# Attention with turned sine weights: TensorE transposes two of a batch's four weight units into the score banks, and the scores accumulate on them

## The chip, the core and the metric

The kernel runs on one NeuronCore of a Trainium2 chip. The metric is device time in microseconds (us) of one execution. Five engines work side by side, each through its own instruction queue in order: TensorE (PE, matmuls and transposes), VectorE (DVE), ScalarE (ACT), GpSimd (POOL) and SyncE (SP, which here only issues DMAs). They meet at semaphores. PSUM, the accumulator memory, has eight banks of 128 x 512 f32.

## What is computed

The input is 16 batches of 256 tokens of width 128. The kernel is one transformer block: attention with eight heads and a second, "quantum" similarity, a small feed-forward part, and a mixture of eight experts behind it. The change touches the attention scores only:

```
qq, kq = Q @ Wc2q + bc2q, K @ Wc2q + bc2q          # 8 numbers per head and token
fid    = (qq @ kq.T) / max(|qq| * |kq|, 1e-8)      # a cosine
qw     = fid * (1 + 0.1 * sin(pi * fid))
cw     = (Q @ K.T) / sqrt(16)
probs  = softmax(0.5 * qw + 0.5 * cw)
heads  = probs @ V
```

## The kernel before

Attention runs batch by batch, 16 times (`batches`). A batch has eight heads, taken two at a time: four units n = 0 to 3, each of them two heads x 256 keys x 256 queries, which is a 128 x 1024 f32 tile. Four such tiles of a batch stand in SBUF as `W[par][:, n, :]` (the trace calls them `big`); `par` is the parity of the batch. Three kinds of unit go through PSUM:

- **max**: Q K^T with queries as rows (`max_unit`, L1210). DVE reduces it over the keys (`top`, L1686), and the row maxima travel over POOL (`split_max`), TensorE (`turn_max`, L1200), ScalarE (`take_max`, L861) and two DMAs into two extra rows of the query stack. Max units belong to the next batch, b + 1.
- **cos**: the cosine, with keys as rows (`cos_unit`, L1328). ScalarE takes the sine into W (L897), DVE forms W = (W + 10) * cos (`weight`, L1735).
- **log**: the score product, keys as rows, with the maxima taken off through the two extra rows (`logit_unit`, L1341). DVE adds W = 0.05 * W + product (`logits`, L1765), ScalarE takes the exponential in place (`exp`, L901), and TensorE multiplies by V (`pv`, L1354, two calls per batch, each on two units of the batch before).

A unit needs two PSUM banks, and there are three such pairs, used in turn: unit number k stands in `slot[k % 3]`. The list `units` fixes the order for a batch b: cos 0, cos 1, cos 2, cos 3, log 0, max 0, log 1, max 1, log 2, log 3, max 2, max 3, with the max units those of b + 1. TensorE waits in `unit` with `pe.wait_ge(unit_free, k - 2)` until DVE has read unit k - 3. Twelve units and three slots: the slot of max 1 is the one of log 0, the slot of max 3 is the one of log 2. The slots of log 0 and log 2 were used before by cos 1 and by max 0.

Each engine's order in a batch is written out by hand (`body` of each engine):

- TensorE: cos 0, 1, 2, `turn_max(b, 1)`, cos 3, `make_qk` for b + 2 (L1180), log 0, max 0, log 1, `turn_u` (L1193), pv 0 of b - 1, max 1, log 2, pv 1 of b - 1, log 3, `turn_max(b + 1, 0)`, `heads_back` (L1366, four 128 x 128 f32 transposes), max 2, max 3.
- VectorE: four weights, then logits 0, top 0, logits 1, top 1, logits 2, logits 3, heads (L1772, L1775), top 2, top 3.
- ScalarE: sin 0, sin 1, `take_max(b, 1)`, sin 2, sin 3, `take_qk` (L848, after `make_qk`), exp 3 of b - 1, exp 0, `take_u`, exp 1, `heads_out` (L906, after pv 1), `take_max(b + 1, 0)` (after log 3 and the transposes of `turn_max` behind it), exp 2. It loads an activation table before the sines and another before the exponentials.
- SP: the DMAs of the maxima, of Q and K (`get_qk`) and of the cosine's operands (`get_u`). Log 0 and log 2 wait for the maxima (`m_in`).

The first batch also has the small weight products of the later parts between its units (`weights_1` to `weights_4`). After the batches come the feed-forward part and the experts, which the change leaves alone. A second copy of the attention loop (`slow`) is for inputs whose norms are tiny; the profiled execution does not take it.

Of the kernel before, what the change touches and what calls it, by code (L numbers as in the profile page):

```python
# [1 line left out]

# [7 lines left out]
ALU = mybir.AluOpType  # L10
ACT = mybir.ActivationFunctionType
# [3 lines left out]
P = 128  # L15
# [6 lines left out]
def bass_sandwich(  # L22
# [8 lines left out]
    NB, S, C = x_d.shape  # L31
    H, _, HD = Wq.shape
    NQ = Wc2q.shape[2]
    FF = W1.shape[1]
    NE, _, EF = ew1.shape
    assert C == P and H * HD == P and S == 2 * P and FF == 4 * P and EF == 4 * P
    TPB = S // P
# [10 lines left out]
    HP = H // 2  # L48
    UW = 2 * TPB * S
    VW = HD + 1  # L50
    KC = 6 * HD
# [11 lines left out]
    with ctx:  # L63
# [8 lines left out]
        slot = [ps[:, 2 * i:2 * i + 2, :].rearrange("p a n -> p (a n)") for i in range(3)]  # L72
# [84 lines left out]
        ident = sb("ident", [P, P])  # L157
# [109 lines left out]
        W = [big[:, i, :, :] for i in range(2)]  # L267
# [134 lines left out]
                    units.append((k, b + d, n))  # L402
        unit_no = {k: i for i, k in enumerate(units)}

        def slot_of(kind, b, n):
            return slot[unit_no[kind, b, n] % 3]

        def batches(eng, body, slow):
            for b in range(NB):
# [169 lines left out]
        def _(pool):  # L579
# [94 lines left out]


            def split_max(b, r):
                pool.wait_ge(unit_free, unit_no["max", b, 2 * r + 1] + 1)
                if b:
                    pool.wait_ge(turn_ps, turn_no[f"m{r}", b - 1] + 1)
                m = mxs[:, b % 2, :, 4 * r:4 * r + 4]  # L680
                nc.gpsimd.tensor_copy(mtok[:, r, :, 0, :], m).then_inc(m_split, 1)  # L681
                pool.wait_ge(m_split, 4 * b + 2 * r + 1)
                nc.gpsimd.tensor_tensor(mtok[:, r, :, 1, :], m, mtok[:, r, :, 0, :], ALU.subtract).then_inc(m_split, 1)
# [129 lines left out]
        def _(act):  # L813
# [71 lines left out]
            def body(b, par, first, last, slow):  # L885
# [11 lines left out]
                    nc.scalar.activation(W[par][:, n, :], src, ACT.Sin, scale=PI * (1 - 1e-6)).then_inc(sin_ready, 1)  # L897

                def exp(b1, par1, n):
                    act.wait_ge(unit_free, unit_no["log", b1, n] + 1)  # L900
                    nc.scalar.activation(W[par1][:, n, :], W[par1][:, n, :], ACT.Exp).then_inc(p_ready, 1)  # L901

                def heads_out(b1):
                    act.wait_ge(pv_done, b1 + 2)
# [230 lines left out]
        def _(pe):  # L1135
# [78 lines left out]
            def unit(kind, b1, n):  # L1214
                k = unit_no[kind, b1, n]
                if k >= 3:
                    pe.wait_ge(unit_free, k - 2)
                return slot[k % 3]

            def weights_1():  # L1220
# [72 lines left out]
            def body(b, par, first, last, slow):  # L1293
                i3 = b % 3

                def guard_unit(n):

                    pe.wait_ge(g_mask, HP * b + n + 1)
                    k = unit_no["cos", b, n] + 1
                    pe.wait_ge(unit_free, k - 2)  # L1300
                    o = slot[k % 3]
                    for h in range(2):
                        for kt in range(TPB):
                            c = (h * TPB + kt) * S
                            mm = nc.tensor.matmul(o[:, c:c + S], g_row[:, S + kt * P:S + (kt + 1) * P],
                                                  g_qrow[:, h * S:(h + 1) * S], start=True, stop=True)
                    mm.then_inc(g_ps, 1)
                    pe.wait_ge(g_min, HP * b + n + 1)

# [11 lines left out]
                def cos_unit(n):  # L1321
                    if n == 0:
                        pe.wait_ge(u_in[par], 80 * (b // 2 + 1))
                    o = unit("cos", b, n)
                    for h in range(2):
                        for kt in range(TPB):
                            c = (h * TPB + kt) * S
                            mm = nc.tensor.matmul(o[:, c:c + S], ukT[par][:, 2 * n + h, kt * P:(kt + 1) * P],  # L1328
                                                  uqT[par][:, 2 * n + h, :], start=True, stop=True)
                    mm.then_inc(unit_ready, 1)  # L1330
                    if slow:
                        guard_unit(n)

                def logit_unit(n):
                    if n % 2 == 0:
                        pe.wait_ge(m_in[n // 2], 16 * (b + 1))
                    o = unit("log", b, n)
                    for h in range(2):
                        for kt in range(TPB):
                            c = (h * TPB + kt) * S  # L1340
                            mm = nc.tensor.matmul(o[:, c:c + S], ckT[i3][0:KC + 2, 2 * n + h, kt * P:(kt + 1) * P],  # L1341
                                                  cqT[i3][0:KC + 2, 2 * n + h, :], start=True, stop=True)
                    mm.then_inc(unit_ready, 1)

                def pv(b1, par1, g):
# [221 lines left out]
        def _(dve):  # L1567
# [72 lines left out]
            for i in range(2):  # L1640
                cp = nc.vector.tensor_copy(bcol_bc[:, i, :], bcol[:, i:i + 1].to_broadcast([P, P]))
            cp.then_inc(set_cp, 1)
            scale = [0.5 / HD ** 0.5, 1.0]
            for i in range(2):
                nc.vector.tensor_scalar(wqk[:, i, :].rearrange("p (d h) -> p h d", h=H), wraw[:, i, :].rearrange("p (h d) -> p h d", h=H),
                                        scale[i], None, ALU.mult)
# [78 lines left out]
            def body(b, par, first, last, slow):  # L1725
# [36 lines left out]

                def logits(n):
                    dve.wait_ge(unit_ready, unit_no["log", b, n] + 1)
                    nc.vector.scalar_tensor_tensor(W[par][:, n, :], W[par][:, n, :], 0.05, slot_of("log", b, n),  # L1765
                                                   ALU.mult, ALU.add).then_inc(unit_free, 1)

                def heads(b1):

# [14 lines left out]
                    weight(n)  # L1784
                if first:
                    own_steps[0] = before_batches
                logits(0)
                if not last:
                    top(b + 1, 0)
                if first:  # L1790
# [3 lines left out]
                    top(b + 1, 1)  # L1794
                if first:
                    root_out(1)
                logits(2)
                if first:
                    weights_3()
                logits(3)  # L1800
                if not first:
# [343 lines left out]
```

## Time and profile before

| | |
|---|---|
| median of 3 runs | 545.84 us (543.92 to 547.48) |
| span of the profiled execution | 546.2 us, 8538 instructions |
| attention batches in the span | from about 68 us to 312 us |
| period of a batch in the middle | 14.24 us (take_qk starts at 215.74 and 229.98) |
| busy: DVE, PE, ACT, POOL | 403.1, 375.6, 343.2, 267.6 us |

The profiled execution has no time of its own beside its span; the span is 0.4 us above the median. In the rows, PE is TensorE's matmuls and PEld its weight loads, each row gives the start or a count, the duration, the engine, the line of the kernel and what it writes and reads. "x4" in a row of the timeline means four instructions merged, and the duration is then that of all of them. Arena, proj and big are names of SBUF areas: "ps<-arena" on L1341 is the score product.

### The profile page before, as it was taken

Reading aid. Unit: us, or ns where it says so; the run is one execution under the profiler, and the core shown is the slowest. Engines: PE = TensorE matmul, PEld = TensorE weight load, DVE = VectorE, ACT = ScalarE, POOL = GpSimd, SP = SyncE. Lnnn points to the kernel's source line nnn. Section 1 sums busy time; section 2 is a strip of 40 time slices with the busy share of each in tenths; the row PEclk is TensorE's granted clock in tenths of the full one; section 3 lists DMA queues with packets and bytes.
Section 4 is the critical chain, followed back from the end, with each engine's and each line's share of the span. In section 5 each row is a group of like instructions: output and inputs, shape, how many; then the busy total and the mean of one; then the engine's idle time right before and its main releaser. Section 6 shows DMA issues by size and latency. Waiting matters only on the chain.

```text
span 546.2 us, 8538 instructions
## 1 busy us (share of the span) xinstructions
PE 375.6 (69%) x2412; PEld 256.7 (47%) x2412; DVE 403.1 (74%) x919; ACT 343.2 (63%) x715; POOL 267.6 (49%) x399
## 2 busy tenths in 40 slices
PE   0958598888778877788777698652000399999960
PEld 0743366554445444445443334552000288888850
DVE  4987658899999999999999623568982026666670
ACT  0234354988988898888988645954300277677740
POOL 8364025444444454444431014274877107777774
PEclk9999956888998899988999989877555589999995
DMA  9461202455555555555551999600111215676600
GB/s 213 28 150 25 61 22 72 106 128 124 134 125 139 138 136 136 125 127 132 133 133 41 136 150 140 197 0 11 41 40 55 75 40 174 192 210 184 171 13 0
DMA packets 81243, 58.16 MB, mean 106 GB/s; under 512 B 17619, under 2 KB 72919, under 8 KB 81196
## 3 DMA queue, kind: packets, MB, share of 16 engines
q1 hardware_dynamic: 75142, 53.12, 43.8%
q0 software_dynamic: 2496, 4.29, 2.4%
q10 hardware_dynamic: 3558, 0.20, 0.5%
q8 instruction: 20, 0.33, 0.3%
q14 instruction: 27, 0.22, 0.2%
HBM read 35.38 MB, written 23.11 MB: 107 GB/s over the span
## 4 chain that ended last, share of the span: by engine, by line
DVE 43%; PE 29%; issue 8%; POOL 8%; ACT 6%; DMA 4%; ACTq 1%; POOLq 0%; DVEq 0%; SPq 0%
DVE mxs L1686 12%; DVE big L1765 11%; DVE big L1735 8%; PE ps L1526 6%; PE ps L1537 5%; POOL sorted_rows L767 4%; DMA x_all<-sorted_rows 2%; PE ps L1180 2%; PE ps L1328 2%; DVE gb L1600 2%; PE ps L1444 1%; POOL late_s L737 1%; PE ps L1449 1%; DMA bc2q_row<-in_L_attn_bc2q_dram 1%; PE ps L1262 1%
## 5 line engine op out<-in xcount | busy, mean ns | idle before, releaser
L1765 DVE SCALAR_TENSOR_TENSOR big<-big,ps 128x1024 f32<-128x1024 f32 x64 | 76.1, 1211 | 5.5 <-PE ps L1341 5.4
L1686 DVE TENSOR_REDUCE mxs<-ps 128x4 f32<-128x1024 f32 x64 | 76.5, 1215 | 2.6 <-issue 1.4
L1735 DVE SCALAR_TENSOR_TENSOR big<-big,ps 128x1024 f32<-128x1024 f32 x64 | 74.7, 1214 | 3.4 <-ACT big L897 3.4
L901 ACT ACTIVATE big<-big 128x1024 f32<-128x1024 f32 x64 | 66.0, 1052 | 6.6 <-DVE big L1765 6.3
L897 ACT ACTIVATE big<-ps 128x1024 f32<-128x1024 f32 x64 | 63.7, 1015 | 9.7 <-PE ps L1328 9.2
L1328 PE MATMUL ps<-proj 128*128 128x256 f16 x256 | 44.0, 303 | 28.9 <-DVE mxs L1686 22.3
L681 POOL CAST mtok<-mxs 128x8 bf16<-128x8 f32 x32 | 6.1, 191 | 102.7 <-DVE mxs L1686 102.7
L2075 DVE TENSOR_SCALAR arena<-ps,x_all 128x128 f32<-128x128 f32 x46 | 14.0, 346 | 57.1 <-PE ps L1546 56.9
L798 POOL DMA_INDIRECT out_dram<-arena,fidx x46 | 46.7, 1016 | 17.6 <-issue 17.3
L1526 PE MATMUL ps<-arena,big 128*128 128x256 f32 x184 | 47.2, 403 | 1.1 <-ACT arena L1106 1.1
L1100 ACT ACTIVATE x_all<-x_all 128x128 f32<-128x128 f32 x46 | 20.1, 487 | 44.2 <-DMA x_all<-sorted_rows 44.0
L1341 PE MATMUL ps<-arena 98*128 98x256 bf16 x256 | 41.7, 289 | 7.3 <-DVE big L1735 4.1
L1328 PEld LDWEIGHTS ps<-proj 128*128 128x128 f16 x256 | 22.2, 105 | 47.0 <-DVE mxs L1686 30.1
L1537 PE MATMUL ps<-arena,big 128*128 128x256 f32 x184 | 43.6, 380 | 0.0
L1210 PE MATMUL ps<-arena 96*128 96x256 bf16 x256 | 38.5, 284 | 5.8 <-DVE mxs L1686 4.2
L1526 PEld LDWEIGHTS ps<-arena,big 128*128 128x128 f32 x184 | 37.0, 202 | 7.3 <-issue 1.9
L767 POOL DMA_INDIRECT sorted_rows<-proj,sl_i x32 | 31.9, 998 | 16.4 <-issue 16.2
L1341 PEld LDWEIGHTS ps<-arena 98*128 98x128 bf16 x256 | 23.0, 105 | 28.0 <-issue 11.8
L1115 ACT ACTIVATE arena<-ps,fbias 128x256 f32<-128x256 f32 x92 | 35.8, 473 | 0.0
L1537 PEld LDWEIGHTS ps<-arena,big 128*128 128x128 f32 x184 | 33.2, 190 | 3.7 <-ACT arena L1115 0.2
L1354 PE MATMUL ps<-big,vb 128*32 128x256 f32 x512 | 34.1, 385 | 0.9 <-DVE u_sb L1775 0.9
L737 POOL TENSOR_TENSOR late_s<-late_s,mhalf 128x16 f32<-128x16 f32 x8 | 23.5, 2942 | 22.3 <-DVE late_s L1824 19.3
(338 smaller groups left out, 883.7 us busy)
## 6 DMA issues: line engine op xcount, KB each, us to landing
big<-in_L_ffn_w_dram SPq DMA_DIRECT2D x46, 256.0 KB, 3.2
qk_parts<-proj SPq DMA_DIRECT2D x16, 384.0 KB, 2.9
arena<-qk_parts SPq DMA_DIRECT2D x32, 192.0 KB, 3.4
sorted_rows<-zrow SPq DMA_DIRECT2D x16, 266.0 KB, 3.5
arena<-qk_parts SPq DMA_DIRECT2D x32, 128.0 KB, 4.0
proj<-u_parts SPq DMA_DIRECT2D x48, 64.0 KB
x_all<-sorted_rows SPq DMA_DIRECT2D x23, 133.0 KB, 2.8
sorted_rows<-zrow SPq DMA_DIRECT2D x2, 1263.5 KB, 24.6
```

The source lines that it names most:

```text
L767: nc.gpsimd.indirect_dma_start(xs_d, bass.IndirectOffsetOnAxis(ap=sl_i[:, t:t + 1], axis=0), srow[:, t, 0:ROW], None).then_inc(scat, 16)
L798: nc.gpsimd.indirect_dma_start(out2, bass.IndirectOffsetOnAxis(ap=fidx[:, j, t:t + 1], axis=0), fres[j][:, t, :], None, bounds_check=NT * ...
L897: nc.scalar.activation(W[par][:, n, :], src, ACT.Sin, scale=PI * (1 - 1e-6)).then_inc(sin_ready, 1)
L901: nc.scalar.activation(W[par1][:, n, :], W[par1][:, n, :], ACT.Exp).then_inc(p_ready, 1)
L1210: mm = nc.tensor.matmul(o[:, c:c + S], cqT[b1 % 3][0:KC, 2 * n + h, qt * P:(qt + 1) * P], ckT[b1 % 3][0:KC, 2 * n + h, :], start=True, sto ...
L1328: mm = nc.tensor.matmul(o[:, c:c + S], ukT[par][:, 2 * n + h, kt * P:(kt + 1) * P], uqT[par][:, 2 * n + h, :], start=True, stop=True)
L1341: mm = nc.tensor.matmul(o[:, c:c + S], ckT[i3][0:KC + 2, 2 * n + h, kt * P:(kt + 1) * P], cqT[i3][0:KC + 2, 2 * n + h, :], start=True, sto ...
L1526: mm = nc.tensor.matmul(ps[:, 1 + 2 * par + c // 2, (c % 2) * TS:(c % 2 + 1) * TS], fw1[j][:, c * P:(c + 1) * P], fxT[par], start=True, st ...
L1537: mm = nc.tensor.matmul(ps[:, 5 + 2 * par, 0:TS], fw2[j][:, c, :], fg[par][:, c, :], start=(c == 0), stop=(c == EC - 1))
L1686: nc.vector.tensor_reduce(mxs[:, b1 % 2, :, 2 * n:2 * n + 2], src, AX_X, ALU.max, negate=True).then_inc(unit_free, 1)
L1735: nc.vector.scalar_tensor_tensor(W[par][:, n, :], W[par][:, n, :], 10.0, f, ALU.add, ALU.mult).then_inc(unit_free, 1)
L1765: nc.vector.scalar_tensor_tensor(W[par][:, n, :], W[par][:, n, :], 0.05, slot_of("log", b, n), ALU.mult, ALU.add).then_inc(unit_free, 1)
```

## The change

Units n = 0 and n = 2 of a batch (`turned_units`) get another path; n = 1 and n = 3 keep theirs.

- For the turned units `cos_unit` swaps its two operands, so that the cosine stands with queries as rows; sine and weight follow with the same instructions.
- `logit_unit` first makes eight 128 x 128 f32 transposes (`is_transpose`, L1367) of W[n] into the score banks, the first of each bank starting it, and then the four score matmuls accumulate on them (`start=False`).
- DVE's `logits(0)` and `logits(2)` are gone. `exp` reads the finished scores from PSUM for these two units and writes W[n].
- The slots of log 0 and log 2 are therefore freed by ScalarE's exponential (`p_ready`), and `slot_free` waits for that. The counts of `unit_free` are kept in `by_dve`.
- The factor 0.05 moves: the query projection is scaled by 20 more, and every exponential has scale=0.05, so `logits` on units 1 and 3 is a plain add.
- The transposes of a unit wait for its slot and for its weights, and stand ahead of the wait for the maxima. `logit_unit` now waits for the slot first and for `m_in` behind it.

```diff
+        turned_units = (0, 2)
+        by_dve = list(itertools.accumulate(k != "log" or n not in turned_units for k, _, n in units))
...
+        def slot_free(eng, k):
+
+            kind, b, n = units[k - 3]
+            if kind == "log" and n in turned_units:
+                eng.wait_ge(p_ready, HP * b + n + 1)
+            else:
+                eng.wait_ge(unit_free, by_dve[k - 3])
...
                 def exp(b1, par1, n):
-                    act.wait_ge(unit_free, unit_no["log", b1, n] + 1)
-                    nc.scalar.activation(W[par1][:, n, :], W[par1][:, n, :], ACT.Exp).then_inc(p_ready, 1)
+                    k = unit_no["log", b1, n]
+                    if n in turned_units:
+                        act.wait_ge(unit_ready, k + 1)
+                        src = slot[k % 3]
+                    else:
+                        act.wait_ge(unit_free, by_dve[k])
+                        src = W[par1][:, n, :]
+                    nc.scalar.activation(W[par1][:, n, :], src, ACT.Exp, scale=0.05).then_inc(p_ready, 1)
...
             def unit(kind, b1, n):
                 k = unit_no[kind, b1, n]
                 if k >= 3:
-                    pe.wait_ge(unit_free, k - 2)
+                    slot_free(pe, k)
                 return slot[k % 3]
...
                     o = unit("cos", b, n)
+                    of_rows, of_cols = (uqT, ukT) if n in turned_units else (ukT, uqT)
...
                 def logit_unit(n):
+                    o = unit("log", b, n)
+                    turn = n in turned_units
+                    if turn:
+                        pe.wait_ge(unit_free, by_dve[unit_no["cos", b, n]])
+                        for h in range(2):
+                            for kt in range(TPB):
+                                for qt in range(TPB):
+                                    to, at = (h * TPB + kt) * S + qt * P, (h * TPB + qt) * S + kt * P
+                                    nc.tensor.matmul(o[:, to:to + P], W[par][:, n, at:at + P], ident[:, :], is_transpose=True,
+                                                     start=(kt == 0 and qt == 0), stop=False, skip_group_check=True)
                     if n % 2 == 0:
                         pe.wait_ge(m_in[n // 2], 16 * (b + 1))
-                    o = unit("log", b, n)
...
-                                                  cqT[i3][0:KC + 2, 2 * n + h, :], start=True, stop=True)
+                                                  cqT[i3][0:KC + 2, 2 * n + h, :], start=not turn, stop=True, skip_group_check=turn)
...
-            scale = [0.5 / HD ** 0.5, 1.0]
+            scale = [20.0 * 0.5 / HD ** 0.5, 1.0]
...
-                    nc.vector.scalar_tensor_tensor(W[par][:, n, :], W[par][:, n, :], 0.05, slot_of("log", b, n),
-                                                   ALU.mult, ALU.add).then_inc(unit_free, 1)
+                    nc.vector.tensor_tensor(W[par][:, n, :], W[par][:, n, :], slot_of("log", b, n), ALU.add).then_inc(unit_free, 1)
...
-                logits(0)
...
-                logits(2)
```

On TensorE, from `make_qk` to `heads_back` of a middle batch, the order before is (L1341 log, L1210 max, L1193 turn_u, L1354 pv, L1200 turn_max, L1366 heads_back):

```order
L1180 MATMUL ps<-xnT,wqk 128x256 x2
L1341 MATMUL ps<-arena 128x256 x4
L1210 MATMUL ps<-arena 128x256 x4
L1341 MATMUL ps<-arena 128x256 x4
L1193 MATMUL ps<-ident_h,proj 128x128 x4
L1354 MATMUL ps<-big,vb 32x256 x8
L1210 MATMUL ps<-arena 128x256 x4
L1341 MATMUL ps<-arena 128x256 x4
L1354 MATMUL ps<-big,vb 32x256 x8
L1341 MATMUL ps<-arena 128x256 x4
```

The same stretch of the changed kernel (lines have moved: L1199 make_qk, L1374 log, L1229 max, L1212 turn_u, L1387 pv; L1367 are the new transposes):

```order
L1199 MATMUL ps<-xnT,wqk 128x256 x2
L1367 MATMUL ps<-ident,big 128x128 x8
L1374 MATMUL ps<-arena 128x256 x4
L1229 MATMUL ps<-arena 128x256 x4
L1374 MATMUL ps<-arena 128x256 x4
L1212 MATMUL ps<-ident_h,proj 128x128 x4
L1387 MATMUL ps<-big,vb 32x256 x8
L1229 MATMUL ps<-arena 128x256 x4
L1367 MATMUL ps<-ident,big 128x128 x8
L1374 MATMUL ps<-arena 128x256 x4
L1387 MATMUL ps<-big,vb 32x256 x8
L1374 MATMUL ps<-arena 128x256 x4
```

Nothing changed places; eight transposes stand ahead of log 0 and eight ahead of log 2, behind max 1.

On VectorE the order of a middle batch before is (L1735 weight, L1765 logits, L1686 top, L1772 and L1775 heads):

```order
L1735 SCALAR_TENSOR_TENSOR big<-big,ps 128x1024 x4
L1765 SCALAR_TENSOR_TENSOR big<-big,ps 128x1024
L1686 TENSOR_REDUCE mxs<-ps 128x2x2
L1765 SCALAR_TENSOR_TENSOR big<-big,ps 128x1024
L1686 TENSOR_REDUCE mxs<-ps 128x2x2
L1765 SCALAR_TENSOR_TENSOR big<-big,ps 128x1024 x2
L1772 RECIPROCAL hsum<-ps 128x16
L1775 TENSOR_TENSOR u_sb<-ps,hsum 128x256
L1686 TENSOR_REDUCE mxs<-ps 128x2x2 x2
```

And in the changed kernel (L1768 weight, L1798 the add of units 1 and 3, L1719 top, L1804 and L1807 heads):

```order
L1768 SCALAR_TENSOR_TENSOR big<-big,ps 128x1024 x4
L1719 TENSOR_REDUCE mxs<-ps 128x2x2
L1798 TENSOR_TENSOR big<-big,ps 128x1024
L1719 TENSOR_REDUCE mxs<-ps 128x2x2
L1798 TENSOR_TENSOR big<-big,ps 128x1024
L1804 RECIPROCAL hsum<-ps 128x16
L1807 TENSOR_TENSOR u_sb<-ps,hsum 128x256
L1719 TENSOR_REDUCE mxs<-ps 128x2x2 x2
```

Two of the twelve large operations of a batch are gone, and top 0 comes straight behind the fourth weight.

## Rows read from the trace of the kernel before

**Rows 1.** The page: busy time and share of each engine; the chain that ended last.

```profile
PE 375.6 (69%) x2412; PEld 256.7 (47%) x2412; DVE 403.1 (74%) x919; ACT 343.2 (63%) x715; POOL 267.6 (49%) x399
DVE 43%; PE 29%; issue 8%; POOL 8%; ACT 6%; DMA 4%; ACTq 1%; POOLq 0%; DVEq 0%; SPq 0%
```

**Rows 2.** Windows: stretch, length, busy us (PE, PEld, DVE, ACT, POOL), PEclk, DMA share, GB/s.

```profile
212.00:226.24 14.24, 10.93 (x98) 6.30 (x96) 14.21 (x15) 12.83 (x17) 6.78 (x12) 1.00 0.53 129
```

**Rows 3.** Lines, 100 to 340 us: count | busy us, mean ns | idle before, releasers.

```profile
L1765 DVE SCALAR_TENSOR_TENSOR big<-big,ps 128x1024 f32<-128x1024 f32 x60 | 71.3, 1210 | 0.5 <-PE ps L1341 0.4
L901 ACT ACTIVATE big<-big 128x1024 f32<-128x1024 f32 x61 | 62.9, 1052 | 4.4 <-DVE big L1765 4.2
L897 ACT ACTIVATE big<-ps 128x1024 f32<-128x1024 f32 x57 | 56.8, 1015 | 2.5 <-PE ps L1328 2.0
```

**Rows 4.** Timeline of a middle batch: start us, duration us, engine, line, operation.

```profile
215.74 0.81 ACT L848 ACTIVATE proj<-ps,qk_col 128x256 f32<-128x256 f32 x2
216.56 1.28 ACT L901 ACT_TABLE_LOAD   x1
217.85 2.00 ACT L901 ACTIVATE big<-big 128x1024 f32<-128x1024 f32 x2
...
219.13 0.61 PE L1210 MATMUL ps<-arena 96*128 96x256 bf16 x4
...
219.72 0.60 PE L1341 MATMUL ps<-arena 98*128 98x256 bf16 x4
...
220.24 1.07 PE L1354 MATMUL ps<-big,vb 128*32 128x256 f32 x16
...
221.25 0.61 PE L1341 MATMUL ps<-arena 98*128 98x256 bf16 x4
...
221.75 2.34 DVE L1765 SCALAR_TENSOR_TENSOR big<-big,ps 128x1024 f32<-128x1024 f32 x2
...
222.63 0.66 PE L1366 MATMUL ps<-ident,hT 128*128 128x128 f32 x4
...
223.13 1.04 PE L1210 MATMUL ps<-arena 96*128 96x256 bf16 x8
...
224.64 2.34 DVE L1686 TENSOR_REDUCE mxs<-ps 128x4 f32<-128x1024 f32 x2
...
227.04 0.19 POOL L681 CAST mtok<-mxs 128x8 bf16<-128x8 f32 x1 [4.09 <-DVE mxs L1686]
...
227.89 0.36 ACT L861 COPY mrow<-ps 8x256 bf16<-8x256 bf16 x1 [0.31 <-PE ps L1200]
...
228.16 1.91 ACT L897 ACTIVATE big<-ps 128x1024 f32<-128x1024 f32 x2
...
229.98 0.81 ACT L848 ACTIVATE proj<-ps,qk_col 128x256 f32<-128x256 f32 x2
```

**Rows 5.** Timeline of the first batch, and windows over it.

```profile
79.54 1.06 PE L1341 MATMUL ps<-arena 98*128 98x256 bf16 x4
...
80.64 1.22 DVE L1765 SCALAR_TENSOR_TENSOR big<-big,ps 128x1024 f32<-128x1024 f32 x1 [3.77 <-PE ps L1341]
...
89.71 1.87 PE L1341 MATMUL ps<-arena 98*128 98x256 bf16 x8
```

```profile
68.00:94.00 26.00, 23.48 (x113) 17.72 (x114) 18.60 (x20) 12.34 (x26) 10.94 (x19) 0.57 0.13 36
```

**Rows 6.** Timeline: four transposes at a lower clock, and what TensorE does next.

```profile
314.22 1.11 PE L1437 MATMUL ps<-ident,u_sb 128*128 128x128 f32 x4 [0.73 <-ACT arena L972]
...
315.13 1.91 PE L1444 MATMUL ps<-arena,wo_c 128*128 128x512 f32 x2
```

**Rows 7.** Timeline of the last batch: the four logits on VectorE.

```profile
303.23 4.60 DVE L1765 SCALAR_TENSOR_TENSOR big<-big,ps 128x1024 f32<-128x1024 f32 x4
```

**Rows 8.** Windows: the four transposes of L1366 at 222.63, and a stretch of lower clock.

```profile
222.63:223.13 0.50, 0.50 (x7) 0.48 (x5) 0.50 (x2) 0.39 (x2) 0.32 (x1) 1.00 0.19 55
...
126.00:129.80 3.80, 3.44 (x14) 2.17 (x15) 3.35 (x4) 3.00 (x4) 2.25 (x5) 0.56 0.65 128
```

More of the change, by code:

```diff
@@ L1 @@
+import itertools
 from contextlib import ExitStack
@@ L676, in split_max @@
             def split_max(b, r):
-                pool.wait_ge(unit_free, unit_no["max", b, 2 * r + 1] + 1)
+                pool.wait_ge(unit_free, by_dve[unit_no["max", b, 2 * r + 1]])
                 if b:
@@ L1299, in guard_unit @@
                     k = unit_no["cos", b, n] + 1
-                    pe.wait_ge(unit_free, k - 2)
+                    slot_free(pe, k)
                     o = slot[k % 3]
                     for h in range(2):
[L1303 to L1306, printed above, removed]
+                        for t in range(TPB):
+                            c = (h * TPB + t) * S
+                            if n in turned_units:
+                                mm = nc.tensor.matmul(o[:, c:c + S], g_qrow[:, h * S + t * P:h * S + (t + 1) * P],
+                                                      g_row[:, S:2 * S], start=True, stop=True)
+                            else:
+                                mm = nc.tensor.matmul(o[:, c:c + S], g_row[:, S + t * P:S + (t + 1) * P],
+                                                      g_qrow[:, h * S:(h + 1) * S], start=True, stop=True)
                     mm.then_inc(g_ps, 1)
@@ L1324, in cos_unit @@
                     o = unit("cos", b, n)
+                    of_rows, of_cols = (uqT, ukT) if n in turned_units else (ukT, uqT)
                     for h in range(2):
[L1326 to L1329, printed above, removed]
+                        for t in range(TPB):
+                            c = (h * TPB + t) * S
+                            mm = nc.tensor.matmul(o[:, c:c + S], of_rows[par][:, 2 * n + h, t * P:(t + 1) * P],
+                                                  of_cols[par][:, 2 * n + h, :], start=True, stop=True)
                     mm.then_inc(unit_ready, 1)
@@ L1796, in body @@
                     root_out(1)
-                logits(2)
-                if first:
                     weights_3()
```

## The prediction

> **What bounds the kernel now.** I began with the page. VectorE is the busiest engine and holds 43% of the chain that ended last [rows 1]. Shares over the whole span say little, so I took one batch from its middle: in 14.24 us VectorE is busy 14.21, ScalarE 12.83, TensorE 10.93 [rows 2]. There VectorE never waits: the 60 score additions on L1765 have 0.5 us of idle time before them in all [rows 3]. A large VectorE operation lasts 1.21 us alone [rows 3], but two in a row take 2.34 [rows 4], so one costs 2.34 - 1.21 = 1.13 us of its time. Twelve of them and the 0.63 us of the heads (from 224.01 to 224.64, that is 221.75 + 2 x 1.13 to the start of the next top [rows 4]) make 14.2: a batch is VectorE's work and nothing else.
>
> **What is taken away.** Two operations of 1.13 us per batch: VectorE's work falls to 14.24 - 2.26 = 11.98 us. The plain add of units 1 and 3 reads the same two operands over the same 1024 columns; no row shows one of that size, so I bound it by 1.13 us as now and by nothing cheaper that would matter, since VectorE would no longer be full. ScalarE keeps its 12.83; an exponential that reads PSUM should last what a sine from PSUM does, 1.015 instead of 1.052 us [rows 3], a gain of 0.04. If the engines only had to be busy, a batch would now take 12.8 us.
>
> **What is added.** Sixteen transposes per batch on TensorE. The nearest row is the same operation on the same shape, four f32 transposes of 128 x 128: they start at 222.63 and the next matmuls start at 223.13 [rows 4], so four cost 0.50 us and eight 1.00. At the lower clock four cost 315.13 - 314.22 = 0.91 [rows 6], and eight 1.82. These are the two bounds; I take 1.00, because the granted clock in the middle batches is 1.00 [rows 2]. TensorE's 10.93 becomes 12.9 of busy time. The swap of the cosine's operands costs nothing: same four matmuls, same columns.
>
> **What is moved, and the loop that it closes.** This decides. Before, VectorE freed every slot. Now max 1 waits until ScalarE has finished exp 0, because log 0 stood in its slot. And exp 0 is late: it stands behind take_qk, the table load and exp 3 of the batch before. In the present trace max 1 starts at 219.13 while exp 0 ends at 217.85 + 2.00 = 219.85 [rows 4]; so it will wait, and log 2 with its eight transposes, pv 1, log 3 and both copies of ScalarE that hang on them are queued behind it on TensorE. I follow that path around once, each stretch from its row in [rows 4]:
>
> - End of top 3 (224.64 + 2.34 = 226.98), over POOL, TensorE and the small copy at 227.89, sines 2 and 3, to take_qk at 229.98: 3.00 us. This stretch is already a chain of waits today.
> - take_qk at 215.74, table, exp 3, exp 0 to its end at 219.85: 4.11.
> - Handing over to TensorE, about 0.05 (226.98 to POOL's start at 227.04 is 0.06).
> - Max 1 to log 2, 219.13 to 219.72: 0.59. Eight transposes: 1.00.
> - Log 2 to pv 1, 219.72 to 220.24: 0.52. pv 1 to log 3, to 221.25: 1.01.
> - Log 3 itself 0.61, and handing over to VectorE 0.05: 0.66.
> - Logits 3, heads, top 2, top 3 without a gap: the second of the pair at 221.75 starts 1.13 later, at 222.88, and top 3 ends at 226.98: 4.10.
>
> Sum: 3.00 + 4.11 + 0.05 + 0.59 + 1.00 + 0.52 + 1.01 + 0.66 + 4.10 = 15.04, and 15.0 with the shorter exponential. Every step must be done once per batch and each needs the one before, so the period cannot be below it. Today the loop does not close: max 1 waits for logits 0 on VectorE, done long before, and not for exp 0, and there are no transposes, so VectorE's 14.24 is the longest way round. So a batch goes from 14.24 to 15.0 us, +0.75, although VectorE does 2.26 us less. VectorE then idles about 3 us per batch, mostly before logits 3.
>
> The other turned unit is harmless. Log 0's transposes need cos 0's weights and its slot, both there while TensorE runs make_qk, and the wait for the maxima now comes behind them. Log 2 frees its slot for max 3 by exp 2; exp 2 is about as late as top 2, which is ahead of top 3 on VectorE, so a wait of TensorE there is covered by 1.13 us of VectorE. Without that cover it would add some 0.3 us per batch.
>
> **The sum.** The 13 full periods in the middle give 13 x 0.75 = 9.8 us. How sure is 0.75? The gaps around pv (0.59, 0.52, 1.01 for work of 0.45 to 0.95) may shrink when TensorE is behind: 0.35 less; then it is +0.4 and 5 us. If the transposes cost half as much again, 0.5 more: +1.25 and 16 us.
>
> The first batch is bound by TensorE and runs at a mean granted clock of 0.57 over 68 to 94 us [rows 5], so nearly always at the lower level of 1.2 GHz. VectorE waits 3.77 us for log 0 there. At that clock eight transposes cost 1.82, twice. With log 0 at 79.54 + 1.82, max 0 one unit (0.85) behind and 1.06 long, top 0 starts at 83.3 instead of some 81.8 (80.64 + 1.13): +1.5. The second group adds 1.8 and saves perhaps 0.6 of the removed logits 2: together +2.8 us, between +1 (transposes at full clock) and +3.6 (nothing saved).
>
> The last batch: VectorE has four logits in a row, 4.60 us [rows 7], and loses two, 2.3 us; TensorE gets 2.0 us of transposes in front of them and pv 1 still stands between log 2 and log 3. I put it at 0, between -2.3 and +2.
>
> 546.2 + 9.8 + 2.8 + 0 = 558.8 for an execution like the profiled one, 558.4 against the median, which lies 0.4 lower. I forecast **558 us**.
>
> **A rule that speaks against it.** The four transposes at 222.63 ran at a granted clock of 1.00, the level of 2.4 GHz [rows 8]. In other batches the clock drops for about 4 us while the sines run: from 126.0 to 129.8 it is 0.56 and VectorE is busy 3.35 of 3.80, so such a dip costs 0.45 us now [rows 8]. Suppose the clock stood at the lower level in every batch while log 2's group runs; it would cost 1.82 in place of 1.00: a period of 15.8 and 546.2 + 13 x 1.6 + 2.8 = 570 us, more if the matmuls around them slow down too. The Trainium skill says this (TensorE: Matmul & The Clock Gate, Part 4: PE-mode transpose): in transpose mode the full clock does not engage. By this rule the time is 570 or above; by the row, where four transposes amid matmuls kept the full clock, it is 558. I follow the row, as matmuls stand on both sides of both groups.
>
> **The rivals.**
>
> - Forecast, the loop over exp 0, log 2 and log 3: 558, own range 551 to 568. Chance 0.62.
> - The loop stays hidden and the change does nothing: the gaps on TensorE shrink and the transposes overlap their neighbours, so that the loop is 14.2 to 14.4 us. For it speaks that 0.8 us is 5% of a chain of some twenty steps. Time: 546.2 + 13 x 0 to 0.15, and 0 to 3 for the first batch: 546 to 551. Chance 0.19.
> - Faster: exp 0 ends before TensorE wants max 1, so ScalarE's 12.8 us sets the period. The point is where take_qk starts: it would have to come 0.7 us earlier relative to max 1. Time: 546.2 - 14 x 1.4 + 2.8 = 529; half of it, 538. Against it stands that take_qk hangs on sin 3 and through it on top 3, which the change makes no earlier. Chance 0.09.
> - The clock falls, or the transposes are slow: 570 to 590. Chance 0.10.
>
> **How the numbers follow.** A difference of 1% (5.5 us) is about what a measurement of this kernel tells from no change. Slower by over 1% (above 551.3): all of the forecast's 0.62 but 0.03, all of the last rival, 0.01 of the second: 0.70. Faster by over 1%: 0.09. The rest, 0.21, is the same. The range 546 to 570 leaves out the faster case and most of the slow transposes, some 0.2.
>
> **What would show it.** In the profile of the changed kernel the period in the middle (take_qk to take_qk) is 15.0 us; VectorE is busy 12 us of it and idles before the add of unit 3, released by log 3 on TensorE; max 1 on TensorE waits for ScalarE's exponential; the eight transposes take 1.0 us at clock 1.00; ScalarE waits before heads_out for pv 1. I am wrong if the period is 14.3 or less, if max 1 shows no wait on ScalarE, or if VectorE is still busy all the time. If the transposes last 1.8 us in the middle, the last rival holds.

## The result, and the profile after

Over 20 runs of each on the same chips the changed kernel takes 550.78 us (548.15 to 553.64), the kernel before 549.31 (543.92 to 554.23). The ratio is 1.0054, with a 95% interval of 1.0030 to 1.0077: by it the change costs about 3 us. I had forecast 558, which is 12 us above the 545.84 of the first three runs of the kernel before (that median was itself low, as the twenty runs show), and a chance of 0.70 for slower by over 1%. The direction was right, the size was not, and the outcome lies in the class "within 1%" to which I gave 0.21. The time lies just under the 551 to 568 of the forecast's own case and inside the 546 to 551 of the second rival, the hidden loop; what follows shows that the loop was not hidden. The profiled execution has a span of 550.9 us, against 546.2.

The page of the changed kernel, busy time and share of each engine, and the chain that ended last:

```profile
PE 393.9 (72%) x2668; PEld 282.0 (51%) x2668; DVE 368.5 (67%) x887; ACT 339.8 (62%) x715; POOL 267.0 (48%) x399
PE 35%; issue 21%; DVE 15%; ACT 14%; SPq 9%; POOL 2%; DMA 2%; ACTq 1%; POOLq 0%; DVEq 0%
```

VectorE does 34.6 us less than in [rows 1] and TensorE 18.3 us more. VectorE's share of the chain falls from 43% to 15%. The work was taken away as intended, and none of it came back as saved time.

Windows of the changed kernel: the first batch, the twelve periods between the second and the last take_qk, and one period of them (stretch, length, busy us of PE, PEld, DVE, ACT, POOL, PEclk, DMA share, GB/s):

```profile
81.56:100.68 19.12, 15.37 (x108) 12.28 (x107) 14.66 (x17) 13.48 (x26) 11.35 (x21) 0.86 0.35 83
100.68:277.81 177.13, 147.58 (x1349) 99.66 (x1348) 144.79 (x144) 152.05 (x193) 81.01 (x144) 1.00 0.52 127
218.78:233.53 14.75, 12.25 (x114) 8.27 (x113) 12.12 (x13) 12.66 (x17) 6.75 (x12) 1.00 0.52 127
```

The same windows of the kernel before, first batch and twelve periods:

```profile
79.78:101.28 21.50, 17.77 (x92) 13.54 (x91) 17.25 (x19) 13.57 (x27) 11.47 (x21) 0.66 0.32 74
101.28:273.25 171.97, 137.63 (x1152) 82.25 (x1150) 170.25 (x168) 154.57 (x193) 81.42 (x144) 0.94 0.53 130
```

A middle batch takes 177.13 / 12 = 14.76 us, and took 171.97 / 12 = 14.33. In it no engine is full: VectorE is busy 12.12 of 14.75 us, ScalarE 12.66, TensorE 12.25. Something that is none of them sets the pace. The first batch became shorter, 19.12 instead of 21.50.

The timeline of one period of the changed kernel shows what (start us, duration us, engine, line, operation, idle time before it and its releaser):

```profile
218.78 0.81 ACT L861 ACTIVATE proj<-ps,qk_col 128x256 f32<-128x256 f32 x2
...
220.90 1.06 ACT L920 ACTIVATE big<-big 128x1024 f32<-128x1024 f32 x1
...
221.86 1.01 ACT L920 ACTIVATE big<-ps 128x1024 f32<-128x1024 f32 x1
...
222.92 0.61 PE L1229 MATMUL ps<-arena 96*128 96x256 bf16 x4 [0.68 <-ACT big L920]
...
223.37 1.04 PE L1367 MATMUL ps<-ident,big 128*128 128x128 f32 x8
...
224.24 0.60 PE L1374 MATMUL ps<-arena 98*128 98x256 bf16 x4
224.78 1.07 PE L1387 MATMUL ps<-big,vb 128*32 128x256 f32 x16
...
225.78 0.61 PE L1374 MATMUL ps<-arena 98*128 98x256 bf16 x4
225.91 0.59 ACT L925 COPY hT<-ps 128x512 f32<-128x512 f32 x1 [1.61 <-PE ps L1387]
...
226.43 1.22 DVE L1798 TENSOR_TENSOR big<-big,ps 128x1024 f32<-128x1024 f32 x1 [1.63 <-PE ps L1374]
...
228.19 2.35 DVE L1719 TENSOR_REDUCE mxs<-ps 128x4 f32<-128x1024 f32 x2
...
233.53 0.81 ACT L861 ACTIVATE proj<-ps,qk_col 128x256 f32<-128x256 f32 x2
```

In order: exp 3 and exp 0 on L920, max 1 (L1229) waiting for exp 0, the eight transposes (L1367), log 2, pv 1 (L1387), log 3, and VectorE idle until log 3 is there. The list of waits between 110 and 280 us says it in sums (waiter, releaser: us in total, times, longest):

```profile
PEld ps L1229 <- ACT big L920: 19.3, 22, 1.2
...
DVE big L1798 <- PE ps L1374: 18.0, 11, 1.6
ACT hT L925 <- PE ps L1387: 17.7, 11, 1.6
```

### The profile page after: what moved, and what is told of

Its sections match the earlier page's. It is cut to its first block, busy times and chain, and to the rows that moved or that the text cites. A ratio compares the mean times of both kernels' runs of the same rounds, so it can differ in the third digit from the quotient of the medians.

```text
span 550.9 us, 9018 instructions
## 1 busy us (share of the span) xinstructions
PE 393.9 (72%) x2668; PEld 282.0 (51%) x2668; DVE 368.5 (67%) x887; ACT 339.8 (62%) x715; POOL 267.0 (48%) x399
## 4 chain that ended last, share of the span: by engine, by line
PE 35%; issue 21%; DVE 15%; ACT 14%; SPq 9%; POOL 2%; DMA 2%; ACTq 1%; POOLq 0%; DVEq 0%
PE ps L1559 8%; DVE mxs L1719 7%; PE ps L1570 7%; ACT big L920 5%; SPq L518 4%; ACT big L910 4%; SPq L557 3%; DVE big L1798 3%; PE ps L1374 3%; PE ps L1367 3%; PE ps L1387 3%; PE ps L1352 2%; PE ps L1229 2%; ACT proj L861 2%; DVE gb L1633 1%
## 5 line engine op out<-in xcount | busy, mean ns | idle before, releaser
L1719 DVE TENSOR_REDUCE mxs<-ps 128x4 f32<-128x1024 f32 x64 | 76.6, 1218 | 21.5 <-PE ps L1229 20.4
L1768 DVE SCALAR_TENSOR_TENSOR big<-big,ps 128x1024 f32<-128x1024 f32 x64 | 74.6, 1216 | 2.5 <-ACT big L910 2.5
L910 ACT ACTIVATE big<-ps 128x1024 f32<-128x1024 f32 x64 | 61.9, 1012 | 7.4 <-PE ps L1352 7.2
L1798 DVE TENSOR_TENSOR big<-big,ps 128x1024 f32<-128x1024 f32 x32 | 38.9, 1216 | 25.5 <-PE ps L1374 25.5
L1352 PE MATMUL ps<-proj 128*128 128x256 f16 x256 | 40.7, 286 | 19.4 <-DVE mxs L1719 14.1
L1229 PE MATMUL ps<-arena 96*128 96x256 bf16 x256 | 39.1, 276 | 18.5 <-ACT big L920 13.9
L1374 PE MATMUL ps<-arena 98*128 98x256 bf16 x256 | 38.7, 275 | 2.7 <-DVE big L1768 2.7
L1229 PEld LDWEIGHTS ps<-arena 96*128 96x128 bf16 x256 | 22.3, 98 | 32.4 <-ACT big L920 24.7
L920 ACT ACTIVATE big<-big 128x1024 f32<-128x1024 f32 x32 | 34.0, 1063 | 2.6 <-DVE big L1798 2.5
L1367 PE MATMUL ps<-ident,big 128*128 128x128 f32 x256 | 34.4, 278 | 1.0 <-DVE big L1768 1.0
L1387 PE MATMUL ps<-big,vb 128*32 128x256 f32 x512 | 34.1, 385 | 1.2 <-DVE u_sb L1807 1.2
```

Of the source, the lines that this page charges most:

```text
L920: nc.scalar.activation(W[par1][:, n, :], src, ACT.Exp, scale=0.05).then_inc(p_ready, 1)
L1229: mm = nc.tensor.matmul(o[:, c:c + S], cqT[b1 % 3][0:KC, 2 * n + h, qt * P:(qt + 1) * P], ckT[b1 % 3][0:KC, 2 * n + h, :], start=True, sto ...
L1352: mm = nc.tensor.matmul(o[:, c:c + S], of_rows[par][:, 2 * n + h, t * P:(t + 1) * P], of_cols[par][:, 2 * n + h, :], start=True, stop=True)
L1367: nc.tensor.matmul(o[:, to:to + P], W[par][:, n, at:at + P], ident[:, :], is_transpose=True, start=(kt == 0 and qt == 0), stop=False, skip ...
L1387: mm = nc.tensor.matmul(hbank[32 * j:32 * j + 32, g * S:(g + 1) * S], vb[:, b1 * TPB + kt, h * VW:h * VW + 32], W[par1][:, h // 2, c:c + S ...
L1719: nc.vector.tensor_reduce(mxs[:, b1 % 2, :, 2 * n:2 * n + 2], src, AX_X, ALU.max, negate=True).then_inc(unit_free, 1)
```

## The experiments

**Theories.** Loop: a batch is one chain around four engines, take_qk, exp 3, exp 0, max 1, transposes, log 2, pv 1, log 3, logits 3, tops, and back over the small copy and the sines. Rival "slots": the harm is only that ScalarE frees slots late. Rival "TensorE's work": sixteen transposes more are too much. For the first batch: clock against VectorE's shorter work against chance. Periods are taken from take_qk to take_qk in the profiled execution. The column "period" has the value that repeats to 0.01 us at full clock; the twelve periods of a trace also hold others, around drops of the clock above all (13.49 to 15.17 in the kernel before), and their mean stands beside it. Ratios are against the kernel before on the same chips; its median there was 549.12 us beside only0, only2 and dbl2, and 547.04 beside the other four edited kernels. The kernel before alone spans 10 us in its twenty runs, so of the single runs only dbl2's time says something.

| kernel | turned units | period us | mean of 12 us | ratio of times, or us |
|---|---|---|---|---|
| before | none | 14.24 | 14.33 | 1 |
| changed | 0, 2 | 14.76 | 14.76 | 1.0054 (1.0030 to 1.0077) |
| only0 | 0 | 14.16 | 14.48 | 0.9895 (0.9854 to 0.9936) |
| only2 | 2 | 14.12 | 14.18 | 0.9937 (0.9886 to 0.9988) |
| dbl2 | 0, 2, log 2's transposes twice | 15.63 | 15.63 | 566.74 us, one run |
| dbl0 | 0, 2, log 0's transposes twice | 14.76 | 14.76 | 549.32 us, one run |
| e0_both | 0, 2, exp 0 ahead of exp 3 | 14.01 | 14.09 | 0.9850 (0.9777 to 0.9924) |
| e0_only0 | 0, exp 0 ahead of exp 3 | 13.42 | 13.73 | 0.9679 (0.9614 to 0.9744) |
| e0_before | none, exp 0 ahead of exp 3 | 14.25 | 14.43 | 548.66 us, one run |

**1. Each group of transposes doubled: dbl2 and dbl0.** The edit, for n = 2, and in the other kernel for n = 0:

```diff
-                        for h in range(2):
+                        for h in [0, 1] * (2 if n == 2 else 1):
                             for kt in range(TPB):
```

> The changed kernel with the transposes ahead of log 2 made twice (the second time over the first, result unchanged). Loop theory: each of them is on the chain, so the period grows by the whole 0.87 us of a group, to about 15.6, and the time by some 12 to 13 us. Rival (VectorE or ScalarE sets the period and TensorE only has less spare time): growth under 0.3 us.

> The changed kernel with the transposes ahead of log 0 made twice, those ahead of log 2 once. Loop theory: log 0's group runs on TensorE while ScalarE goes through take_qk, the table load and exp 3, and is off the chain; the period stays within 0.2 us of 14.76, while the same doubling ahead of log 2 gave 15.63. Rival, TensorE's total work: 15.6 here too.

Doubling log 2's group makes every period 0.87 us longer, 14.76 to 15.63, which is what eight transposes take. The timeline of dbl2, sixteen transposes and VectorE's wait for log 3, and its window over one period:

```profile
229.49 1.91 PE L1367 MATMUL ps<-ident,big 128*128 128x128 f32 x16
...
233.42 1.22 DVE L1798 TENSOR_TENSOR big<-big,ps 128x1024 f32<-128x1024 f32 x1 [2.50 <-PE ps L1374]
```

```profile
224.90:240.53 15.63, 13.13 (x122) 9.14 (x121) 12.13 (x13) 12.66 (x17) 6.75 (x12) 1.00 0.49 120
```

VectorE's wait grows from 1.63 to 2.50, by the same 0.87. Doubling log 0's group costs nothing. The timeline of dbl0, the doubled group and max 1, and its window:

```profile
215.75 1.91 PE L1367 MATMUL ps<-ident,big 128*128 128x128 f32 x16
...
220.38 0.61 PE L1229 MATMUL ps<-arena 96*128 96x256 bf16 x4 [0.18 <-ACT big L920]
```

```profile
216.24:230.99 14.75, 12.97 (x122) 9.24 (x121) 12.22 (x13) 12.75 (x17) 6.77 (x12) 1.00 0.53 127
```

The extra time went into TensorE's wait for exp 0: 0.18 us of matmul idle time are left of 0.68. TensorE is busy 12.97 us per batch in dbl0 and 13.13 in dbl2, nearly the same, yet one costs nothing and the other 0.87 us. "TensorE's work" has fallen; the place of the work decides.

**2. One unit turned instead of two: only0 and only2.** The turned unit alone takes the new path, and the other's logits stand again on VectorE where they stood:

```diff
-        turned_units = (0, 2)
+        turned_units = (0,)
...
                 if first:
                     root_out(1)
+                logits(2)
+                if first:
                     weights_3()
```

> Only unit 0 of a batch is turned; unit 2 goes over VectorE as before. Loop theory (the batch is set by the chain take_qk, exp 3, exp 0, max 1, log 2, pv 1, log 3, logits 3, tops): max 1 still waits for exp 0, but the eight transposes ahead of log 2 (0.87 us) are gone, while logits 2 comes back onto VectorE. Period in the middle about 13.9 to 14.1 us, against 14.76 with both units turned and 14.24 before. Rival, slots alone (whatever ScalarE frees late costs the time, transposes are covered): the wait for exp 0 is the whole harm, so the period stays at about 14.7. Rival, VectorE's work alone: 14.24 - 1.13 = 13.11.

> Only unit 2 of a batch is turned. Loop theory: max 1 waits for logits 0 on VectorE as in the kernel before and no more for exp 0; log 2's transposes are in a shorter chain from top 0. Period about 13.9 to 14.1 us. Rival, slots alone: slot of max 3 is freed by exp 2, covered, so VectorE's 13.11 us would set it. Rival, TensorE's work alone: half of the rise from 14.24 to 14.76, so 14.5.

At 14.16 and 14.12 they lie 0.06 and 0.02 above the loop theory's range, and farther from the rivals' 14.5, 14.7 and 13.1. In only0 the slot is still freed by exp 0, and max 1 waits for it as in the changed kernel; but without the transposes log 3 is early enough that VectorE runs top 1, logits 2 and logits 3 back to back. From the timeline of only0:

```profile
217.98 0.61 PE L1229 MATMUL ps<-arena 96*128 96x256 bf16 x4 [0.67 <-ACT big L920]
...
218.62 1.23 DVE L1719 TENSOR_REDUCE mxs<-ps 128x4 f32<-128x1024 f32 x1 [0.95 <-PE ps L1229]
...
219.77 2.34 DVE L1798 TENSOR_TENSOR big<-big,ps 128x1024 f32<-128x1024 f32 x2
```

So by the timeline the way around is another one than the expectation named (no run tests this separately). It turns off at max 1: 4.09 us from take_qk (213.84) to the end of exp 0, 0.05, 0.64 to top 1, 1.15 to logits 2, 5.23 from there to the end of top 3 (225.00), and 3.00 to the next take_qk (228.00), together 14.16. Over log 2, pv 1 and log 3 it would be the 14.75 of the changed kernel less 0.87, that is 13.88.

In only2 max 1 does not wait, and the transposes still make VectorE wait for log 3, 0.91 us where it was 1.63:

```profile
217.01 0.61 PE L1229 MATMUL ps<-arena 96*128 96x256 bf16 x4
...
217.51 1.09 PE L1367 MATMUL ps<-ident,big 128*128 128x128 f32 x8
...
220.62 1.22 DVE L1798 TENSOR_TENSOR big<-big,ps 128x1024 f32<-128x1024 f32 x1 [0.91 <-PE ps L1374]
```

Here the transposes wait for top 0, which frees the slot of log 2 (its end, 216.24 + 1.22 = 217.46), and the loop is top 0, transposes, log 2, pv 1, log 3, logits 3 and VectorE's work back to the next top 0, without ScalarE's exponentials in it.

So the slot freed late and the transposes are each bearable: either alone leaves a batch a little shorter than before where the clock is full (with four drops of the clock in its trace, only0's mean of 14.48 is not shorter). They stand in series on one chain, and together they make it 14.76. "Slots" alone has fallen too.

**3. The chain cut: e0_both, e0_only0 and the control e0_before.** ScalarE does exp 0 first:

```diff
-                if not first:
-                    exp(b - 1, 1 - par, HP - 1)
                 for n in range(HP - 1):
                     exp(b, par, n)
+                    if n == 0 and not first:
+                        exp(b - 1, 1 - par, HP - 1)
...
-                eng.wait_ge(p_ready, HP * b + n + 1)
+                eng.wait_ge(p_ready, HP * b + n + (1 if n or not b else 0))
...
-                    pe.wait_ge(p_ready, HP * b1 + 2 * g + 2)
+                    pe.wait_ge(p_ready, HP * b1 + 2 * g + 2 + (1 if g and b1 < NB - 1 else 0))
```

> The changed kernel (both units turned), and on ScalarE exp 0 of a batch stands ahead of exp 3 of the batch before instead of behind it, with the counts that are waited for shifted accordingly; everything is computed. Loop theory: exp 0, which frees max 1's slot, comes one exponential (0.95 us) earlier; pv 1, which needs exp 3, is no later than log 2 before it. The period falls from 14.76 by 0.6 to 0.8 us, to 14.0 to 14.1 us. Rival (TensorE's sixteen transposes are simply too much work next to the rest): no change, 14.7 us.

> Only unit 0 turned, and exp 0 ahead of exp 3 of the batch before on ScalarE. Loop theory: the chain of 14.16 us that only unit 0 gave loses one exponential and something else closes at about 13.4 to 13.5 us; VectorE's own work of 13.1 is close behind. The time falls to about 533 to 537 us, the best of all versions so far. Rival (some other chain already stands at 14.1, since turning unit 0 alone and unit 2 alone gave 14.16 and 14.12): 14.1 us.

> The kernel before with nothing turned, and exp 0 ahead of exp 3 on ScalarE. Control: VectorE's twelve operations set the period, so it stays at 14.24 where the clock does not drop. Rival (the order of the exponentials costs time of itself, and the gain of the other two runs has nothing to do with the slot): it moves by over 0.3 us.

All three periods came out as the loop theory had them; the time of e0_only0 is 1.3 us below its range. e0_both: 14.76 to 14.01, with TensorE's work untouched. Its timeline shows log 1, pv 0, max 1, the transposes and logits 3:

```profile
212.22 0.61 PE L1374 MATMUL ps<-arena 98*128 98x256 bf16 x4 [0.22 <-DVE big L1768]
...
212.99 1.07 PE L1387 MATMUL ps<-big,vb 128*32 128x256 f32 x16
...
213.99 0.61 PE L1229 MATMUL ps<-arena 96*128 96x256 bf16 x4
...
214.44 1.04 PE L1367 MATMUL ps<-ident,big 128*128 128x128 f32 x8
...
217.50 1.22 DVE L1798 TENSOR_TENSOR big<-big,ps 128x1024 f32<-128x1024 f32 x1 [1.63 <-PE ps L1374]
```

Exp 0 now ends at 213.73, and max 1 follows pv 0 without waiting for it. What closes at 14.01, by the timeline, is the next loop: weight 3 on VectorE frees the slot of log 1 (212.22), then turn_u, pv 0, max 1, the transposes, log 2, pv 1, log 3, logits 3, and VectorE's run to the next weight 3. So the swap paid 0.75 us of an exponential's 0.95, and the transposes are still on the way around.

e0_before: 14.25 in the periods at full clock, so the order of the two exponentials is worth nothing by itself. e0_only0 is the best kernel of this study, 531.69 us against 547.04 on the same chips. Its timeline and window:

```profile
211.40 1.03 ACT L920 ACTIVATE big<-ps 128x1024 f32<-128x1024 f32 x1
...
212.68 0.61 PE L1229 MATMUL ps<-arena 96*128 96x256 bf16 x4
...
213.33 1.23 DVE L1719 TENSOR_REDUCE mxs<-ps 128x4 f32<-128x1024 f32 x1 [0.21 <-PE ps L1229]
```

```profile
209.28:222.70 13.42, 11.30 (x106) 7.42 (x105) 13.18 (x14) 12.82 (x18) 6.76 (x12) 1.00 0.57 140
```

Max 1 no longer waits. VectorE is busy 13.18 of 13.42 us and is again nearly the engine that sets the pace (14.24 less one operation of 1.13 us is 13.11); the row of top 1 shows 0.21 us of waiting for max 1. Not every period of this kernel is 13.42, and the mean is 13.73. Two drops of the clock lengthen some, and two at full clock last 13.80 and 14.14: in them log 0 waits for the DMA of the maxima. (The kernel before has such waits too, 0.57 us at 201.72 in a period of 14.25, where VectorE's work covers them.)

```profile
182.41 0.61 PE L1374 MATMUL ps<-arena 98*128 98x256 bf16 x4 [0.54 <-DMA arena<-m_parts]
...
196.56 0.61 PE L1374 MATMUL ps<-arena 98*128 98x256 bf16 x4 [0.89 <-DMA arena<-m_parts]
```

**4. The first batch: b_dummy, first_old, before_again, after_again.** b_dummy adds to the kernel before, in its first batch alone, work that nothing reads:

```diff
                     o = unit("log", b, n)
+                    if first and n % 2 == 0:
+                        for i in range(8):
+                            nc.tensor.transpose(o[:, i * P:(i + 1) * P], ident[:, :], ident[:, :])
```

first_old is the changed kernel with nothing turned in its first batch (`b > 0 and n in (0, 2)` in place of `n in turned_units`). The other two are the two kernels once more, without an edit.

> The kernel before, and in its first batch alone eight transposes of the identity into the score banks ahead of log 0 and of log 2, which the score products then overwrite; nothing else changes. Tests why the first batch got shorter (take_qk to take_qk 21.50 us before, 19.12 in the changed kernel). Clock theory: the added matmul work brings TensorE to its full clock earlier, so the weight products at L1245 take about 1.1 us instead of 2.06 and the first batch is not longer than 21.5 although 3 us of work was added. Rival (the first batch got shorter because VectorE does two operations less, 2.3 us): here it gets longer, by 1 to 3 us.

> The changed kernel with the first batch left as it was before (nothing turned in it), batches 1 to 15 as changed. Clock theory for the first batch: without transposes ahead of its log 0 the granted clock between the first and the second take_qk stays at about 0.66, as in the kernel before (0.66, first batch 21.50 us), the weight products of 128x128 take 2.06 us and the first batch lasts 21 us or more, against 0.86, 1.14 us and 19.12 us in the changed kernel. Rival (the first batch got shorter because VectorE does two operations less): it must be longer too, but at a clock and with weight products as in the changed kernel. Rival (chance from run to run): no relation. Period in the middle 14.76 by every theory.

> The kernel before once more, for a second trace of the same program. Both theories: 14.24 us per batch where the clock does not drop. It shows how far the start (first take_qk at 79.78) and the first batch (21.50 us, clock 0.66) move by themselves: clock theory 0.66 again, chance 0.6 to 0.9.

> The changed kernel once more, for a second trace. Loop theory: the period is 14.76 again in every batch, since no step of the chain depends on chance. Clock theory: the first batch is at 0.75 or more and lasts 19 to 20 us. Chance: like the kernel before.

| kernel | transposes ahead of log 0 of the first batch | clock | first batch us |
|---|---|---|---|
| before, before_again | no | 0.66, 0.58 | 21.50, 22.09 |
| e0_before, only2 | no | 0.66, 0.66 | 20.84, 22.76 |
| first_old | no | 0.58 | 20.09 |
| changed, after_again | yes | 0.86, 0.86 | 19.12, 19.13 |
| dbl2, dbl0 | yes | 0.95, 0.85 | 18.78, 19.80 |
| only0, e0_only0 | yes | 0.74, 0.76 | 19.89, 20.35 |
| e0_both, b_dummy | yes | 0.81, 0.83 | 21.57, 20.81 |

b_dummy's window over its first batch, and the weight products of L1245, at the level of 2.4 GHz (the same products took 2.06 us in the trace of the kernel before):

```profile
81.10:101.91 20.81, 16.57 (x108) 12.63 (x107) 16.02 (x19) 13.36 (x27) 11.50 (x21) 0.83 0.30 73
```

```profile
87.99 1.14 PE L1245 MATMUL ps<-big 128*128 128x128 f32 x8
```

Sixteen transposes of about 3 us that nobody needs were added, and the first batch did not get longer, 20.81 against 21.50, 22.09 and 20.84. TensorE was even busy for less of it, 16.57 us with 108 matmuls against 17.77 with 92. The granted clock parts the thirteen executions without overlap: 0.58 to 0.66 where TensorE has nothing ahead of log 0, 0.74 to 0.95 where it has. That much of the clock theory held. Its finer claims did not: first_old has a clock of 0.58 as expected, but lasts 20.09 us and not 21, and its weight products took 1.14 us, since the low stretch lay elsewhere. The first batch's time scatters by some 2 us at one clock (22.09 and 20.09 at 0.58), so that the clock can account for added work that costs nothing there, and not for each single time. How much of the changed kernel's 19.12 us comes from VectorE's two missing operations these runs do not show: b_dummy, which has the transposes and keeps the two operations, took 20.81.

The two repeats show what is firm. In after_again the middle periods are 14.75 to 14.79, as in the first trace. In before_again they are 13.84 to 15.16, mean 14.47, where the clock drops. The clock of its first batch was 0.58 and not the expected 0.66.

## Why the prediction was right or wrong

**Which steps failed.** The mechanism held and the sizes did not. I had put the change at +12.6 us on the profiled execution, 9.8 for the middle and 2.8 for the first batch; the profiled pair gave +4.7, and the ratio of the twenty runs about 3. Three terms failed: the loop's sum, 15.04 us where the same steps measured 14.75; the batch that it was compared with, 14.24 where the mean was 14.33; and the first batch, +2.8 where the traces show -2.4.

**What was right.** VectorE stopped being the bound and idles before logits 3; the loop that I followed exists, step by step; log 0's transposes are covered; the slot of max 3 costs nothing (top 2 and top 3 run without a gap at 228.19). The clock did not fall: 1.00 over all twelve middle periods with sixteen transposes in each. That is a measurement against the rule of the Trainium skill (TensorE: Matmul & The Clock Gate, Part 4: PE-mode transpose) that the full clock does not engage in transpose mode, at least where matmuls stand around the transposes.

**The loop's sum, 15.0, was about 0.25 us too long.** By the same steps in the changed kernel: 2.99 from the end of top 3 to take_qk (I had 3.00), 4.09 to the end of exp 0 (4.11 less 0.03), 0.05 handing over, 0.45 for max 1 (0.59), 0.87 for the transposes (1.00), 0.54, 1.00, 0.65 and 4.11 (0.52, 1.01, 0.66, 4.10). Two of its steps were mis-sized. The 0.59 behind max 1 was read off a stretch that included a gap of TensorE's (its matmuls need 0.45); that gap was absent where TensorE had waited for exp 0. The transposes were priced by doubling the 0.50 of a row of four. Four took 0.49 in the changed kernel too (226.55 to 227.04), but eight in a row took 0.87, 0.109 each: what four cost beyond 4 x 0.109 does not double. Why is not shown. Over 13 periods these 0.25 us are 3 us.

**The period before was not 14.24 everywhere.** Seven dips of the clock had put the twelve periods at a mean of 14.33. I had named a dip's price, 0.45 us [rows 8], and then compared my loop with a batch without one. In the changed kernel there are no dips in the middle. This is another 0.09 us per batch, about 1 us. The price was wrong as well: twelve times 14.24 is 170.88, so seven dips cost 1.1 us, 0.16 each; where two follow each other, three periods (158.28 to 201.49) last 43.21 in place of 42.72, 0.25 each. So the twelve periods gave +5.2 us (177.13 - 171.97) where 12 x 0.75 = 9.0 was forecast. Against the second trace of the kernel before, mean 14.47, it is 3.5.

**The first batch had the wrong sign.** I charged two groups at the lower clock, +2.8 us. In the profiled pair it is -2.4, in the repeats -3.0 (19.13 and 22.09). In the changed kernel's timeline the first group took 1.91 us, and the second 1.07, for the clock had risen in between:

```profile
81.32 1.91 PE L1367 MATMUL ps<-ident,big 128*128 128x128 f32 x8
...
89.53 1.07 PE L1367 MATMUL ps<-ident,big 128*128 128x128 f32 x8
```

I priced added work at the clock of a stretch whose clock depends on that work, as b_dummy shows (0.83 with the work, 0.58 to 0.66 without). My lower bound for it, +1, did not allow for this either.

**The last batch** was well put at 0: from the last take_qk to the last heads, a stretch that also holds the thirteenth period, it is 39.45 in the changed kernel and 38.81 before, +0.6.

The account of the profiled pair: start of the program +1.8, first batch -2.4, middle +5.2, last stretch +0.6, expert part -0.5, in all +4.7. Two of these terms are scatter: the first take_qk starts between 75.97 and 81.56 us in the thirteen traces, and what follows the last heads, which no edit touches, took between 229.8 and 235.5. So a single pair of spans tells 5 us from nothing only by its middle.

This also bears on the kernels with one unit turned, whose ratios are more than their periods explain. In only0's trace the span is 6.1 us shorter than before, although the twelve periods are 1.8 us longer; 4.1 of it lie behind the last heads and 3.6 ahead of the second take_qk. In e0_only0's, 15.2 us shorter, the periods and the last stretch give 8.9, and 4.1 again lie behind the last heads. That part took 229.8 to 230.0 us in the three kernels with one unit turned, and 230.7 to 235.5 in the other ten traces. What links it to the edit no run here shows.

## What to carry to other kernels

Taking work from the busiest engine helps only until the longest way around through all engines closes; before the edit, walk that way once from rows, and look at what the edit adds to it in series: here a slot freed by a late exponential and 0.87 us of transposes, each harmless alone, together worse than nothing. When a buffer's release moves to another engine, move that engine's releasing instruction to the front of its queue in the same edit: with that swap, and one unit turned instead of two, the same idea was 3% faster than the kernel before, in the profiled pair somewhat over half of it from the batches themselves. Each such cut uncovers the next bound (by the timelines, 14.16, 14.01 and 13.42 us were each set by another one), so walk the way around again after every edit.

Work on TensorE that is priced in a stretch of low clock may cost nothing there (16 transposes in b_dummy), and a comparison needs the mean period with its dips, not the clean one.

## What was not expected of the hardware

Eight f32 transposes of 128 x 128 in a row, each with its own weight load, took 0.87 us at the full clock from their start to the next matmul, 0.109 us each, and sixteen took 1.75 (229.49 to 231.24 in dbl2). In the first batch the mean granted clock was 0.58 to 0.66 in the five traces without transposes ahead of log 0, and 0.74 to 0.95 in the eight with them.

In the middle batches it mattered where the transposes stand. The drops of the clock during the sines, seven in the trace before, are gone in all seven traces with unit 2 turned, only2 among them: from the second of the twelve periods on each has a clock of 1.00. With unit 0 alone turned, the same number of transposes, they are still there: 0.85 to 0.93 in four periods of only0, 0.86 and 0.88 in two of e0_only0. These traces show that and not why.
